# Two buffers of a feed-forward stage placed 32 bytes further in each partition

## The reference

```python
x = x + xattn(layernorm(x), ctx, ctx, Wq, Wk, Wv, Wo)      # 32 heads of 32, 8 key/value heads
h = layernorm(x)
g, u = h @ dequant(w1).T, h @ dequant(w3).T                # 1024 -> 3584, twice
x = x + (silu(g) * u) @ dequant(w2).T                      # 3584 -> 1024
```

## The kernel before

| tensor | starts at | remainder by 128 | one matmul reads |
|---|---|---|---|
| `q_w_h`, `q_w_l` (stationary) | 51776, 84544 | 64, 64 | 512 bytes, at multiples of 512 from the start |
| `q_xT_h`, `q_xT_l` (moving) | 133856, 162528 | 96, 96 | 1792 bytes, at multiples of 1792 (14 x 128) |
| `m_w_h`, `m_w_l` (moving) | 116288, 149056 | 64, 64 | 2048 bytes |
| `g_WH`, `g_WL` (stationary) | 80448, 94784 | 64, 64 | 512 bytes, at multiples of 512 |
| `g_XH`, `g_XL` (moving) | 116288, 166464 | 64, 64 | up: 1792 bytes, at multiples of 1792; down: 2048 bytes |
| `g_su`, `g_Sh` | 216640, 222016 | 64, 64 | |

## Time and profile before

### The profile page before, as it was taken

How to read it: one execution, slowest core, us unless ns; L and a number is a source line. 1 busy time by engine, 2 the same in 40 slices (tenths; PEclk the granted TensorE clock), 3 DMA queues, 4 the chain that set the end, 5 groups by cost and what they waited for, 6 DMA issues and landing times.

```text
span 2511.5 us, 35414 instructions
## 1 busy us (share of the span) xinstructions
PE 2424.5 (97%) x12682; PEld 2069.3 (82%) x12682; DVE 1727.6 (69%) x2639; ACT 979.1 (39%) x1673; POOL 576.1 (23%) x305
## 2 busy tenths in 40 slices
PE   7998999999999699799999999999999989999999
PEld 7997878878876388699999988998899978888887
DVE  6425777777776446788888889898889874445442
ACT  3212445444454422444444445344443342323221
POOL 1000354454454400011111111332333320000000
PEclk9998999999998799899999999999999999999999
DMA  7534555455545345465655554666676687565652
GB/s 225 174 96 135 146 135 146 131 142 143 133 113 130 86 155 168 126 203 168 186 170 168 165 151 148 181 180 183 194 211 182 172 284 228 170 186 151 186 163 84
DMA packets 369146, 408.04 MB, mean 162 GB/s; under 512 B 125824, under 2 KB 324096, under 8 KB 359152
## 3 DMA queue, kind: packets, MB, share of 16 engines
q1 hardware_dynamic: 369008, 406.22, 56.7%
HBM read 252.99 MB, written 152.70 MB: 162 GB/s over the span
## 4 chain that ended last, share of the span: by engine, by line
PE 44%; DVE 9%; issue 3%; DMA 2%; ACT 0%; DVEq 0%; ACTq 0%
PE bank L84 15%; PE bank L85 15%; PE bank L86 15%; DVE g_WL L90 2%; DMA stash<-weight_scratch 2%; DVE g_su L1731 1%; DVE stash L1736 1%; DVE g_XL L90 1%; DVE stash L1228 1%; DVE stash L1226 1%; DVE xT L1723 1%; DVE stash L1225 1%; DVE stash L1249 0%; ACT g_XH L1659 0%; ACT g_WH L1198 0%
## 5 line engine op out<-in xcount | busy, mean ns | idle before, releaser
L84 PE MATMUL bank<-g_XH,g_WH 128*128 128x448 f32 (+1 forms) x2254 | 847.1, 376 | 30.2 <-DVE g_XL L90 15.9
L86 PE MATMUL bank<-g_XH,g_WL 128*128 128x448 f32 (+1 forms) x2254 | 845.0, 375 | 0.0
L85 PE MATMUL bank<-g_XL,g_WH 128*128 128x448 f32 (+1 forms) x2254 | 844.9, 375 | 0.0
L84 PEld LDWEIGHTS bank<-g_XH,g_WH 128*128 128x128 f32 x2254 | 424.5, 188 | 93.7 <-DVE g_WL L90 18.1
L86 PEld LDWEIGHTS bank<-g_XH,g_WL 128*128 128x128 f32 x2254 | 424.6, 188 | 55.3
L85 PEld LDWEIGHTS bank<-g_XL,g_WH 128*128 128x128 f32 x2254 | 424.7, 188 | 54.3
L90 DVE TENSOR_TENSOR g_WL<-stash,g_WH 128x512 fp32r<-128x512 f32 (+1 forms) x417 | 349.3, 841 | 75.8 <-ACT g_WH L1198 47.1
L1198 ACT ACTIVATE g_WH<-stash 128x512 fp32r<-128x512 f32 x392 | 241.7, 628 | 398.9 <-PE bank L86 245.1
L696 DVE TENSOR_REDUCE a_nm<-bank 112x1 f32<-112x375 f32 x512 | 264.9, 531 | 117.1 <-PE bank L831 113.8
L800 ACT ACTIVATE a_pr<-bank 125x448 f32<-125x448 f32 x384 | 204.0, 545 | 204.4 <-PE bank L907 150.8
L649 POOL TENSOR_TENSOR a_prsum<-a_pr 125x1792 f32<-125x1792 f32 x32 | 129.3, 4042 | 363.0 <-ACT a_pr L800 363.0
(11 more groups left out here) (132 smaller groups left out, 3617.8 us busy)
## 6 DMA issues: line engine op xcount, KB each, us to landing
stash<-in_L_ffn_w SPq DMA_DIRECT2D x168, 256.0 KB, 5.2
weight_scratch<-stash SPq DMA_DIRECT2D x28, 1024.0 KB, 7.6
stash<-weight_scratch SPq DMA_DIRECT2D x28, 1024.0 KB, 5.4
h_scratch<-g_Sh SPq DMA_DIRECT2D x112, 224.0 KB, 2.8
down_scratch<-xT SPq DMA_DIRECT2D x98, 256.0 KB, 3.0
stash<-in_ctx SPq DMA_DIRECT2D x48, 500.0 KB
stash<-h_scratch SPq DMA_DIRECT2D x25, 896.0 KB, 6.4
a_qst<-q_scratch SPq DMA_DIRECT2D x96, 224.0 KB, 4.7
```

The source lines that it names most:

```text
L84: pe.matmul(acc, lh, rh, start=first, stop=False, skip_group_check=onto)
L85: pe.matmul(acc, lh, rl, start=False, stop=False, skip_group_check=onto)
L86: return pe.matmul(acc, ll, rh, start=False, stop=last, skip_group_check=onto)
```

## The change

One allocation is added ahead of the two moving-operand buffers, of 8 float32 values (32 bytes) in each partition. Nothing reads or writes it. `g_XH`, `g_XL`, and behind them `g_su` and `g_Sh`, start 32 bytes further: their remainder by 128 goes from 64 to 96. Every instruction is the same but for these addresses. `g_WH`, `g_WL`, `g_t1`, `stash` and `xT` stay where they are, and so does all of the stages before.

```diff
                 W_AT = {9: (0, 1), 10: (2, 3), 11: (4, 5), 12: (6,)}
                 mixing(xT, Ahead)
+                sb("lead", [P, 8])
                 XH, XL = sb("XH", [P, 7, KH, TB], f32r), sb("XL", [P, 7, KH, TB], f32r)
                 su, Sh = sb("su", [P, 3, TB]), sb("Sh", [P, 4, TB])
```

## The result

The changed kernel is slower: 2522.92 us, median of 9 runs (2510.23 to 2529.48), against 2510.01 us for the kernel before (9 runs, 2502.25 to 2513.42). The ratio is 1.0056, 95% interval 1.0038 to 1.0073. The forecast was 2491, its range 2484 to 2515; rival B, which loses its lock in the down products, had 2524.5.

A forecast was written before the change was run, and what follows sets the result against it. The prediction took TensorE's matmul pitch as the bound. Up products would gain 15.0 us in steps 0 to 27 and 4.4 in 28 to 55, down products and writes nothing: 19.4 us, so 2491 us, range 2484 to 2515.

The forecast's parts named there:

- rival B: Down products: the 512-column streams lose their lock and fall to 233.3 ns, 13.7 us more, 2524.5 us in total; chance 0.12.
- What bounds the kernel: Whole kernel: TensorE, busy 97% of 2511.5 us; a nanosecond less per matmul is worth one wherever TensorE waits for nothing.
- By the lowest seven bits, just the layout of the queries: Up products: the change gives them the queries' address layout, so their pitch goes from 206.7 to 200 ns.
- Term 4: Down products: stay at 226.7 ns, nothing gained; bounds one 16-cycle step each way, 13.7 us less or more.
- Step 1: Up products, steps 0 to 27: matmuls go from 206.56 to 200 ns, 15.0 us gained after 0.2 given back.
- Step 2: Up products, steps 28 to 55: VectorE's additions hold back most of 11.2 us, leaving 4.4 us gained.
- Term 5: ScalarE and VectorE writes, now to remainder 96: cost taken as 0, bounds 0 to 1.3 us.
- The spread should shrink: Whole kernel: the 8.8 us spread of three runs, which the two up pitches can make, should shrink.
- Rival A: Whole kernel: the 32 bytes do nothing, say 2511 us; cited the attention's key projection, tiles 1504 bytes apart, no pattern; chance 0.27.

The follow-up runs named there:

- the map: Probe tables of matmul pitch by d, the moving operand's start less the stationary one's, by 256 bytes: 448 columns 200.0 to 206.7 ns, 512 columns 226.7 to 236.6.
- the kernel with d 64: Against the kernel before: up products' moving operands 64 bytes past the stationary ones, down products at distance 0; 0.9983, 2500.74 us against 2505.35.
- small sums: GpSimd's down-weight sums cut to 32 columns of 512: steps 28 to 55 fall from 496.1 to 474.4 us (d 64 kernel), 496.5 to 489.1 (kernel before).
- the probes: Three kernels with only TensorE bursts of 84 matmuls and ScalarE copies, varying operand distance, stalls and load width; 512 columns: 226.7 ns at distance 0, 233.3 at 32.

## Why the prediction was wrong

What bounds the kernel: right, a nanosecond on each matmul is one on the path, wherever TensorE doesn't wait. The down stage is the proof: 2058 x 6.6 ns = 13.6 us, and 13.4 came.

"By the lowest seven bits, just the layout of the queries": the step that failed for the up products. The period is 256, not 128, and d 32 is another place than 160. It isn't a place without the fast lock either: 200.0 is there at 32, as one of three. In the profiled run of the changed kernel it held only in the stretch after step 27. The forecast took one reading at one distance as the value of an address; the two pitches of the kernel before, which it named itself, should have warned that an address gives a set of locks.

Term 4, the down products at nothing: the step that cost the range. The argument was that columns + 32 cycles is the lowest pitch of the rows, so nothing could be gained. It says nothing of what can be lost, and a stage at the best value of its kind can only lose by a move. The bound of one 16-cycle step was the exact size: 6.6 ns, in part by luck, since other distances cost 2.2 to 7.6. Rival B named the mechanism, its price (13.7 us, measured 13.4), the duration (396, measured 395) and the total (2524.5, measured 2522.92), and got 0.12. Its reason, the other half of a 64-byte piece, was not it: at d 64, in the same half, 512 columns have 228.9 ns, and with both operands moved by 32 bytes 226.7. With the map, of the seven other multiples of 32 none leaves 512 columns at 226.7.

Step 1, steps 0 to 27 at 15.0 us: not realised by the change (496.9 before, 497.0 after), but with 200 ns in every step it is 12.7 (the kernel with d 64). The slack of VectorE held in steps 6 to 22, as said, but not around them: step 4 gave back 1.3 us and not 0.2, and the waits in steps 24 and 27 grew by 0.5 and 0.4. And this count is from one execution in the slowest lock of d 0; the forecast knew that the address has two pitches and still took the gain of the profiled execution for that of the median.

Step 2, steps 28 to 55 at 4.4 us: the mechanism was right and the size off: 0.4 with a pitch of 200. The three sub-products outside VectorE's run of 25 us did not keep their gain; 1.5 us went to the lower clock behind step 32's longer stall, and where the rest went is open. In all whole kernels run here but those with small sums these steps take 492.2 to 496.5 us, at pitches from 200.0 to 206.7. Small sums free them. So the sum for the fast lock would have been 13.1, not 19.4 us, against the profiled execution, and 4.6 between the medians.

Term 5, the writes: right at nothing. The addition into `g_su` takes 610 ns for 609.

"The spread should shrink": wrong, it grew to 19 us. At d 32 the locks lie up to 6.7 ns apart, at d 0 4. With a distance of one lock it does shrink, to 4 us. That the locks make the spread fits this but is not shown, since one execution of each kernel has a trace.

Rival A's reason from the attention was no evidence, though not for the cause it gave (too few matmuls in a row): the probes' bursts of 448 columns at d 32 are in their lock from the third distance on. Its tiles, 1504 bytes apart, are 32 short of a multiple of 256, so no distance lasts longer than one tile.

## What to carry to other kernels

Where weight load and matmul alternate back to back, the distance of the two operands' starts by 256 bytes is here worth 3 to 4% of each matmul (f32r, loads of 128 columns; no other type was run). The best one depends on the number of columns, so stages that share a buffer may want different offsets in it. Moving an allocation can change that distance with no instruction changed: keep both operands' remainders in view when a buffer is resized, and measure at the new distance before trusting a pitch read at another. Take a pitch from several stretches after different stalls and from many runs: one trace can show one of several locks.

## What was new about the hardware

- A stream of 512 f32r columns with loads of 128 repeats every 226.7 to 236.6 ns, one of 448 every 200.0 to 206.7 ns, by the distance of the operands' starts, at the full clock and with all other engines idle; 256 bytes further the pitch is the same.
- Some distances have more than one stable pitch (448 columns at 32: 200.0, 204.5, 206.7), kept for up to some 2000 matmuls and changed only at a stall. What chooses one is open.
- A matmul with fewer weight columns can be slower: 512 moving columns at distance 0 take 226.7, 229.8 and 231.6 ns with 128, 64 and 32.
